# A four-layer stack conditioned on a vector: the lead-in in another order, the keys third, and one reciprocal of the softmax sums per batch

## The chip, the core and the metric

The kernel runs on one core of a Trainium2 chip. The metric is the device time in microseconds. Three runs of the kernel before took 2391.41, 2392.73 and 2393.94 us; the median is 2392.73. All numbers of the trace are from one more execution, the profiled one, of 2394.26 us.

## The reference

x is 4 batches of 512 tokens by 512 channels, with one conditioning vector a batch. Four layers follow each other, all in float32.

```
cond @ W            # 12 blocks of 512 columns: scales and shifts of all layers
layer 0: h = layernorm(x) * (1 + scale) + shift
         q = h Wq (16 heads of 32); c = h Wkd (128); k, v = c Wku, c Wvu (4 heads, each shared by 4)
         rotate q and k; mask: own block of 128, window of 64, every 64th token, no later block
         x += softmax(q k / sqrt(32)) v @ Wo
layer 1: rms norm * scale; 8 heads of 64, one k and v; rotate; no mask; x += attention @ Wo
         x += (silu(h Wg) * (h Wu)) Wd       # 2048 wide
layer 2: 16 heads of 32, normed q and k, added mask; then a GELU MLP, both gated by cond
layer 3: 8 small expert MLPs side by side, norm, silu, output projection
```

## The kernel before

Everything is held with channels (or head channels) on the 128 partitions and tokens along the free axis: a tensor of one batch is four tiles of 128x512. `C`, `TT` and `B` are all 4.

**One woven order.** The program has no loops at run time. Python builds one list of operations (stage, batch, engine, kind, index); each engine runs its own part of the list strictly in order (`Woven`) and waits on the other engines' counters by position. Three parts of it matter here. `lead` holds everything before the first score. `attention01` (`weave`) is the attention of layers 0 and 1, in eight mains: layer 0 for batches 0 to 3, then layer 1. `weave` goes through quads of four score units (16 quads to a batch of layer 0, 8 of layer 1): scores on TensorE into banks 0 to 3, mask and maximum on VectorE (L815), exponential on ScalarE (L845), then transposes ("turn", L909 and L911, in layer 1 L743) into banks 4 and 5, two copies to SBUF on ScalarE (L850) and two on VectorE (L822), and values (L926, L929) into bank 6. Each quad has four points. At them side operations are let in by `sides01`: what prepares the next batch (norm, projections L407, rotations) and the output projection of the last one, spread evenly over the points of the batch.

**Spreading the softmax sums.** After two groups of values, one tile of 128 channels holds four heads (in layer 1 two) and has to be divided by each head's sum. VectorE takes the reciprocals of 16 (8) columns (L827, "recip"). TensorE then makes them a 128x512 tile ("spread", L769): for every block of 128 tokens and every head one full-precision product of a column, broadcast to 32 (64) weights, with the identity. VectorE multiplies (L833, "divide"). This is done four times per batch. A spread takes the next of banks 4 and 5, as a turn does, so the turn after next waits for the divide.

**The lead-in.** `ada` computes the conditioning: 12 blocks (L132; each weight block of 1 MB goes into one of three buffers), a copy of the row on ScalarE (L152), a product that turns it to columns ("turn", L138) and an addition on VectorE (L167). `angles` computes layer 1's rotation tables from the positions: 14 operations on VectorE (L79 to L91), a sine and a cosine on ScalarE (L98). `norm0` is the layer norm of a batch: two sums on GpSimd (L281), the third (L290), a mean on TensorE (L268), centring (L347), squares (L306), sums (L285, L290), variance (L268), logarithm and root (L314, L319), scale (L367) and shift (L331). `proj0` has eight groups: latent, q0 to q3, v, k, near values. `rope0` rotates the key tile and four q tiles: in batch 0 through a product with a permutation (L457), later by two DMAs of SP a tile ("swap", L1885), then a product with the sine on VectorE (L472), one with the cosine and a sum on GpSimd (L484, L490). The list is: angles first; then the whole norm; then blocks 0 and 1 and their turns, and the other blocks folded among projections and rotations.

**Queues.** SP issues in order: block 0, x of batch 0, blocks 1 to 3, block 4, x of batch 1 and so on, each block from the fourth on waiting until TensorE has used the block three before. Then for each batch (b > 0) the swaps of keys and q0, 15 copies that lay the four key heads out to four tiles of four equal strips (L1897), and the swaps of q1 to q3. The first score of a batch waits for all 15 (`k_loaded`). GpSimd issues first: positions, identity and small tables, the biases, layer 0's weights and its rotation tables; then it computes.

## Time and profile before

| | |
|---|---|
| Median of three runs | 2392.73 us |
| Profiled execution, its time | 2394.26 us |
| Its span, first to last instruction | 2392.5 us |
| Busy: TensorE, VectorE, ScalarE, GpSimd | 94%, 49%, 43%, 12% |
| First score | 93.27 us |
| First score of layer 1 | 439.12 us |

The span is the distance between the first and the last instruction on any engine. A full-precision matmul stands as two records; the end of a matmul is modelled, so consecutive ones overlap in the records, and start to start is what one costs in a stream. PE is TensorE, PEld its weight loads, DVE VectorE, ACT ScalarE, POOL GpSimd; a q behind a name is its sequencer. PEclk is the clock that TensorE was granted, as a share of 2.4 GHz. "[7.32 <-DVE sb_nmax L815]" behind a row says that the engine had been idle for 7.32 us before it and that VectorE's L815 ended that.

### The profile page before, as it was taken

What the parts mean: (1) busy time and instruction counts of PE and PEld (TensorE: products, weight loads), DVE (VectorE), ACT (ScalarE), POOL (GpSimd) and SP (SyncE); (2) the same over time, 40 slices, a digit from 0 to 9 for tenths busy, and PEclk for the clock granted to TensorE, in tenths of its full rate; (3) what the DMA queues carried; (4) which work ended last, traced back from release to release, by engine and by line L of the source; (5) the groups of instructions that cost most, each with busy time, mean ns of one, the idle gap of its engine ahead of it and who ended that gap; (6) DMA issues with size and microseconds to landing.
All of it is one profiled execution on the core that took longest, in us unless ns stands there. A gap on an engine that the chain in (4) does not pass through costs nothing.

```text
span 2392.5 us, 34589 instructions
## 1 busy us (share of the span) xinstructions
PE 2246.8 (94%) x14034; PEld 1510.8 (63%) x14034; DVE 1171.0 (49%) x2499; ACT 1034.0 (43%) x2425; POOL 291.3 (12%) x246
## 2 busy tenths in 40 slices
PE   5889999999999999999999989999999899999998
PEld 2455555555555688888887756565654578888633
DVE  2345454454457344443443366667587554544322
ACT  2355555444446221111113266667576552222473
POOL 3331122122021000010000010101010110000021
PEclk9889999999999999999999999999999999999999
DMA  8310020000010002110102211011110101100001
GB/s 275 113 40 27 15 62 28 22 24 18 19 41 27 31 27 84 63 53 27 36 6 82 77 61 64 27 63 36 54 37 19 35 19 36 36 1 1 1 18 53
DMA packets 59487, 104.97 MB, mean 44 GB/s; under 512 B 10592, under 2 KB 24560, under 8 KB 59328
## 3 DMA queue, kind: packets, MB, share of 16 engines
q1 hardware_dynamic: 58368, 100.30, 12.6%
q0 software_dynamic: 960, 2.45, 0.3%
q8 instruction: 111, 1.82, 0.3%
q14 instruction: 48, 0.39, 0.1%
HBM read 77.04 MB, written 10.49 MB: 37 GB/s over the span
## 4 chain that ended last, share of the span: by engine, by line
PE 84%; ACT 7%; DVE 6%; POOL 1%; issue 1%; SPq 1%; DMA 1%; DVEq 0%; POOLq 0%; ACTq 0%
PE banks L1218 36%; PE banks L407 22%; PE banks L743 6%; PE banks L735 4%; PE banks L759 4%; ACT sb_Pr L845 2%; PE banks L769 2%; PE banks L268 2%; ACT sb_PT L850 1%; PE banks L909 1%; DVE sb_hN L367 1%; PE banks L633 1%; PE banks L641 1%; DVE sb_Pr L815 1%; PE banks L893 1%
## 5 line engine op out<-in xcount | busy, mean ns | idle before, releaser
L1218 PE MATMUL banks<-sb_HH,sb_Ws 128*128 128x512 f32 x1536 | 489.4, 392 | 7.6 <-DVE sb_HL L1106 7.6
L1218 PEld LDWEIGHTS banks<-sb_HH,sb_Ws 128*128 128x128 f32 x1536 | 289.3, 188 | 71.2 <-issue 8.1
L1218 PE MATMUL banks<-sb_hidH,sb_Ws 128*128 128x512 f32 x1024 | 330.3, 392 | 0.4 <-DVE sb_x L1289 0.4
L845 ACT ACTIVATE sb_Pr<-sb_Pr,sb_nmax 128x512 f32<-128x512 f32 (+4 forms) x512 | 291.7, 577 | 31.8 <-DVE sb_nmax L815 31.7
L1218 PE MATMUL banks<-sb_HL,sb_Ws 128*128 128x512 f32 x768 | 299.7, 390 | 0.0
L850 ACT ACTIVATE sb_PT<-banks 128x512 f32<-128x512 f32 (+2 forms) x320 | 143.6, 496 | 303.3 <-PE banks L743 226.8
L822 DVE COPY sb_PT<-banks 128x512 f32<-128x512 f32 (+2 forms) x320 | 168.6, 564 | 163.6 <-PE banks L743 109.8
L743 PEld LDWEIGHTS banks<-sb_ident,sb_Pr 128*128 128x128 f32 x1536 | 168.9, 142 | 126.3 <-issue 40.0
L743 PE MATMUL banks<-sb_ident,sb_Pr 128*128 128x128 f32 x1536 | 213.6, 281 | 18.4 <-DVE sb_A L833 5.0
L1218 PEld LDWEIGHTS banks<-sb_hidH,sb_Ws 128*128 128x128 f32 x1024 | 192.2, 188 | 43.8 <-issue 2.3
L1218 PE MATMUL banks<-sb_hidL,sb_Ws 128*128 128x512 f32 x512 | 199.3, 389 | 0.0
L407 PE MATMUL banks<-sb_A,sb_W 128*128 128x512 f32 x384 | 176.6, 603 | 3.8 <-DVE sb_x L1493 2.4
L815 DVE CUSTOM_DVE_ANT_0 sb_Pr<-banks,sb_bias 128x512 f32<-128x512 f32 x256 | 161.5, 687 | 34.5 <-PE banks L735 34.1
L1270 DVE TENSOR_TENSOR sb_tiles<-sb_tiles,banks 128x512 f32<-128x512 f32 x64 | 44.0, 688 | 256.0 <-PE banks L1218 256.0
L1245 ACT ACTIVATE sb_hidH<-sb_tiles 128x512 fp32r<-128x512 f32 x128 | 81.0, 633 | 197.3 <-DVE sb_tiles L1270 195.3
L1218 PEld LDWEIGHTS banks<-sb_HL,sb_Ws 128*128 128x128 f32 x768 | 145.0, 189 | 30.6 <-issue 1.0
L407 PE MATMUL banks<-sb_hN,sb_W 128*128 128x512 f32 x320 | 150.4, 614 | 4.9 <-ACT sb_hN L331 2.8
L735 PE MATMUL banks<-sb_R 32*128 32x512 f32 (+1 forms) x768 | 143.6, 636 | 1.7 <-DVE sb_R L594 0.8
L1240 ACT ACTIVATE sb_tiles<-banks,sb_cols 128x512 f32<-128x512 f32 x64 | 44.1, 689 | 232.2 <-PE banks L1218 232.1
L1289 DVE SCALAR_TENSOR_TENSOR sb_x<-banks,sb_mod,sb_x 128x512 f32<-128x512 f32 x128 | 95.7, 750 | 91.2 <-PE banks L1218 90.9
L1237 ACT ACTIVATE sb_tiles<-banks 128x512 f32<-128x512 f32 x64 | 38.2, 598 | 213.8 <-PE banks L1218 213.8
L759 PE MATMUL banks<-sb_PT,sb_V 128*32 128x256 f32 (+1 forms) x1536 | 127.0, 393 | 0.0
(160 smaller groups left out, 3217.4 us busy)
## 6 DMA issues: line engine op xcount, KB each, us to landing
sb_ring<-split_units SPq DMA_DIRECT2D x48, 512.0 KB, 3.3
sb_ropet<-sb_R SPq DMA_DIRECT2D x70, 128.0 KB, 2.0
sb_staged<-in_L_cond_Wfc SPq DMA_DIRECT2D x16, 512.0 KB, 4.6
sb_wada<-in_L_cond_Wada SPq DMA_DIRECT2D x6, 1024.0 KB, 5.6
split_units<-sb_unitpair SPq DMA_DIRECT2D x12, 512.0 KB, 2.9
sb_x<-in_x SPq DMA_DIRECT2D x4, 1024.0 KB, 9.1
sb_staged<-in_L_cond_Wg SPq DMA_DIRECT2D x8, 512.0 KB, 3.7
sb_staged<-in_L_cond_Wu SPq DMA_DIRECT2D x8, 512.0 KB, 4.7
```

Source lines behind the costliest of these rows:

```text
L268: e.matmul(bank, k.ones[:], k.t1[:, 0, :], start=True, stop=True).then_inc(k.done["pe"], 1)
L407: mm = e.matmul(out, lhsT, rhs, start=start, stop=stop)
L735: mm = e.matmul(bank[:, 0:s.width(u)], s.q(b, c)[rows, i * P:(i + 1) * P], s.k(b, c)[rows, 0:s.width(u)], start=True, stop=True)
L743: mm = e.transpose(bank[:, j * P:(j + 1) * P], k.Pr[:, n % 6, j * P:(j + 1) * P], k.ident[:])
L759: mm = e.matmul(bank[rows, 2 * P * ip + skip:2 * P * (ip + 1)], s.v(b, j, s.vhead(c, hl)), s.PT[:, n % 2, hl, j, skip:2 * P], start=j == 0 ...
L815: ins = e.tensor_tensor_reduce(k.Pr[:, n % 6, 0:s.width(u)], S, s.bias[:, s.units[u][2], 0:s.width(u)], -1.0, 3.0e38, ALU.add, ALU.min, s. ...
L822: ins = e.tensor_copy(*s.turned(k, b, u))
L845: ins = e.activation(prob, prob if s.biased else k.bank(n % 4)[:, 0:s.width(u)], ACT.Exp, bias=s.stat(k, k.nmax, b, u), scale=-1.0 if s.bi ...
L850: ins = e.activation(*s.turned(k, b, u), ACT.Copy)
L1218: mm = e.matmul(bank, lhsT, rhs, start=i == 0, stop=i == len(mats) - 1)
L1245: ins = e.activation(k.hidH[:, st % 2, t, :], k.tile(t), ACT.Copy)
L1289: ins = e.scalar_tensor_tensor(out=k.xs(q, m), in0=s.tab.at[(s.name, b, "down", index)], scalar=1.0 if s.gamma is None else s.gamma(q, m), ...
```

## The change

**Order of the lead-in.** The list is now: sums and block 0; mean; block 1 and turn 0; variance sums; turn 1; block 2; variance; scale and shift; the angle reduction; then a chain of 13 pieces (latent, q0, key, q1, rotation of the key with the sine and cosine tables, q2, rotation of q0, q3, rotation of q1, v, rotation of q2, near values, rotation of q3) with blocks 3 to 11 folded among them. SP loads x of batch 0 first, then blocks 0 and 1, layer 0's weights (before on GpSimd's queue), block 2, the rotation tables (before on GpSimd's queue), the mask, and later blocks; blocks 8 to 11, x of batches 2 and 3 and further weights are issued after batch 0's key copies. The biases have a semaphore of their own, which only the first turn's addition waits for.

**Keys third.** `keys_first` puts the key product third and the key's rotation sixth among the pieces that prepare batches 1 to 3 of layer 0.

**Scores wait by key tile.** There is a semaphore for each of the four key tiles; the first unit of each tile waits for its own copies.

**Reciprocals once per batch.** In layer 0 (all batches) and layer 1 (batches 0 and 1), "recip" and "spread" go. After the last unit of a batch VectorE takes one reciprocal of all 64 (32) columns ("recips") and splits it in a rounded part and the rest. One quad later TensorE transposes the two, 32 columns in all, for each block of tokens ("rows", four transposes), ScalarE copies the 32x512 result as float32r ("rows copy"), and TensorE makes each 128x512 tile by one single-pass product with 32 rows ("wide"): tiles 0 and 1 at the end of that quad, 2 and 3 in the middle of the next. Both kinds use banks 4 and 5. The matrix for it is one more small load (`headsel`), rounded in the lead-in.

```diff
+        elif kind == "rows":
+            for due in after(s.name, b, "rest", 4 // s.per - 1):
+                e.wait_ge(*due)
+            bank = s.tab.claim(e, s, b, kind, u, after)
+            for i in range(TT):
+                columns = k.inverses[:, i, :, :].rearrange("p v h -> p (v h)").bitcast(F32)
+                mm = e.transpose(bank[0:32, i * P:(i + 1) * P], columns, k.ident[:])
+        elif kind == "wide":
+            for due in after("headmatrix", 0, "round", 0):
+                e.wait_ge(*due)
+            for due in after(s.name, b, "rows copy", 0):
+                e.wait_ge(*due)
+            bank = s.tab.claim(e, s, b, kind, u, after)
+            mm = e.matmul(bank, k.headsel[0:32, u, :], k.rows[0:32, :], start=True, stop=True)
...
+        elif kind == "recips":
+            for due in after(s.name, b, "exp", s.U - 1):
+                e.wait_ge(*due)
+            ins = e.reciprocal(k.rsum[:, b % 2, 0:s.U], k.sums[:, b % 2, 0:s.U])
+        elif kind in ("rounded", "rest"):
+            per_row = 4 // s.per
+            for due in after(s.name, b, "recips", 0):
+                e.wait_ge(*due)
...
+                    e.wait_ge(*due)
+            src = k.rsum[:, b % 2, 0:s.U].rearrange("p (c i h) -> p i c h", c=C, i=TT)
+            out = [k.inverses[:, :, v, :].rearrange("p i (c h d) -> p i c h d", c=C, h=s.per)[:, :, :, :, u]
+                   for v in range(2)]
+            if kind == "rounded":
+                ins = e.tensor_copy(out[0], src)
+            else:
+                ins = e.tensor_tensor(out[1], src, out[0].bitcast(F32), ALU.subtract)
...
-            for due in after(s.name, b, "spread", u):
-                e.wait_ge(*due)
-            ins = e.tensor_tensor(s.out(b, u), s.out(b, u), s.tab.at[(s.name, b, "spread", u)], ALU.mult)
+            spread = "wide" if b in s.whole else "spread"
+            for due in after(s.name, b, spread, u):
+                e.wait_ge(*due)
+            ins = e.tensor_tensor(s.out(b, u), s.out(b, u), s.tab.at[(s.name, b, spread, u)], ALU.mult)
...
+        elif kind == "rows copy":
+            for due in after(s.name, b, "rows", 0):
+                e.wait_ge(*due)
...
+            ins = e.activation(k.rows[0:32, :], s.tab.at[(s.name, b, "rows", 0)][0:32, :], ACT.Copy)
...
-            if u == 0:
-                e.wait_ge(*s.k_loaded(b))
+            if u % (s.U // C) == 0:
+                e.wait_ge(*s.k_loaded(b, c))
...
+        for h, b, c in wide[3:]:
+            seq.extend([(h, b, "pe", "wide", c), (h, b, "dve", "divide", c)])
+        wide, later = later, []
+        for h, b, c in wide[:1]:
+            seq.extend([(h, b, "pe", "rows", 0), (h, b, "act", "rows copy", 0)])
         for h, b, u in units(t - 1)[3:]:
             if (u + 1) % h.G == 0:
                 g = h.group(u)
                 seq.append((h, b, "pe", "values", g))
                 if g % 2:
-                    seq.extend([(h, b, "act", "out", g // 2), (h, b, "dve", "recip", g // 2)])
+                    seq.append((h, b, "act", "out", g // 2))
+                if g % 2 and b not in h.whole:
+                    seq.append((h, b, "dve", "recip", g // 2))
                     spreads.append((h, b, g // 2))
+                if b in h.whole and (u + 1) == h.U:
+                    seq.append((h, b, "dve", "recips", 0))
+                    seq.extend((h, b, "dve", kind, i) for kind in ("rounded", "rest") for i in range(4 // h.per))
+                    later = [(h, b, c) for c in range(-1, C)]
...
+        for h, b, c in wide[1:3]:
+            seq.extend([(h, b, "pe", "wide", c), (h, b, "dve", "divide", c)])
...
+                       whole=(0, 1, 2, 3))
...
+                       whole=(0, 1))
...
-        start = pre(0, 0, 1, 2)
...
-        lead = [(ada, 0, "act", "silu", 0), (angles, 0, "dve", "reduce", 0), (angles, 0, "act", "sin", 0),
-                (angles, 0, "act", "cos", 0), (angles, 0, "dve", "negate", 0)] + start[0] + sum(blocks[:3], []) + \
-            fold(start[1:], (0, len(start) - 1, blocks[3:])) + [(ada, 0, "act", "scales", 0)] + \
-            [(ada, 0, "dve", "comb", i) for i in range(len(combs))]
+        def keys_first(proj, rope):
+            return [proj[i] for i in (0, 1, 6, 2, 3)] + rope[:1] + [proj[i] for i in (4, 5, 7)], rope[1:]
+        n0, (p0, r0) = pre(0, 0), keys_first(pre(0, 1), pre(0, 2))
+        headmatrix = HeadMatrix(headsel_read, (l_sel, 16))
+        table = [(angles, 0, "act", "sin", 0), (angles, 0, "act", "cos", 0), (angles, 0, "dve", "negate", 0)]
+        chain = [p0[0], p0[1], p0[2], p0[3], p0[5] + table, p0[4], r0[0], p0[6], r0[1], p0[7], r0[2], p0[8], r0[3]]
+        lead = [(ada, 0, "act", "silu", 0)] + \
+            sum([n0[0], blocks[0], n0[2], blocks[1], n0[3], blocks[2], blocks[3], n0[5], n0[6]], []) + \
+            [(angles, 0, "dve", "reduce", 0)] + fold(chain, (0, 12, blocks[4:])) + \
+            [(ada, 0, "act", "scales", 0)] + [(ada, 0, "dve", "comb", i) for i in range(len(combs))] +             [(headmatrix, 0, "dve", "round", 0)]
         sides01 = []
         for m in range(2 * B - 1):
-            late = beats(posts[m - 1]) if m else []
-            sides01.append(([] if m else pre(1, 0)) + pre(m + 1, 1) + among(late, pre(m + 1, 2), pre(m + 2, 0)) + [[]])
+            late = [[]] * (m > 3) + beats(posts[m - 1]) if m else []
+            first, rest = keys_first(pre(m + 1, 1), pre(m + 1, 2)) if m < 3 else (pre(m + 1, 1), pre(m + 1, 2))
+            sides01.append(([] if m else pre(1, 0)) + first + among(late, rest, pre(m + 2, 0)) + [[]])
...
-            for n, (name, j) in enumerate(blocks):
+            def load_x(b):
+                e.dma_start(x[:, :, b, :], xrows[:, :, b, :]).then_inc(l_x[b], 16)
+            def load_block(n):
+                name, j = blocks[n]
                 if n >= 3:
                     done("ada", 0, "block", n - 3)
                 e.dma_start(wada[n % 3][:], rows(name)[:, :, j * D:(j + 1) * D]).then_inc(l_ada[n % 3], 16)
...
+            load_x(0)
+            load_block(0)
+            load_block(1)
+            for dst, name in ((wkd, "L0_cond_Wkd"), (wq0, "L0_cond_Wq")):
+                e.dma_start(dst, rows(name)).then_inc(l_w[0], 16)
+            for dst, name in ((wku, "L0_cond_Wku"), (wvu, "L0_cond_Wvu")):
+                e.dma_start(dst, a[name]).then_inc(l_w[0], 16)
+            load_block(2)
+            for dst, name in ((perm, "perm"), (k.cosr, "cos0"), (k.sinr, "sin0")):
+                e.dma_start(dst[:], a[name]).then_inc(l_rope, 16)
+            e.dma_start(mask_own[:], a["mask0"][0:P, 0:P]).then_inc(l_bias[0], 16)
+            e.dma_start(mask_near[:], a["mask0"][P:].rearrange("(i p) t -> p i t", p=P)).then_inc(l_bias[0], 16)
+            load_block(3)
+            for name, _ in COLS:
+                e.dma_start(col[name], a[name]).then_inc(l_cols, 16)
+            e.dma_start(k.smul[:], a["L2_cond_scale_mul_log"]).then_inc(l_cols, 16)
+            e.dma_start(k.strip[:], a["strip"]).then_inc(l_cols, 16)
+            e.dma_start(headsel_read[0:32], a["headsel"]).then_inc(l_sel, 16)
+            for n in (4, 5):
+                load_block(n)
+            load_x(1)
+            for n in (6, 7):
+                load_block(n)
...
-                    if c == C - 1:
-                        e.wait_ge(l_k, 16 * (15 * b + 12))
+                    for before in range(C - 1) if c == C - 1 else ():
+                        e.wait_ge(l_k[before], 64 * (b + 1))
                     for strip in range(4 if c < C - 1 else 3):
                         e.dma_start(k.R[32 * strip:32 * strip + 32, b % 2, 1, c, :], heads[32 * c:32 * c + 32, :])\
-                            .then_inc(l_k, 16)
+                            .then_inc(l_k[c], 16)
                 for g in range(2, 5) if b else ():
                     swap(rope0, b, g)
+                if b == 0:
+                    for n in range(8, len(blocks)):
+                        load_block(n)
+                    load_x(2)
+                    load_x(3)
...
-                e.dma_start(modb[:, t0:t0 + n], a[name]).then_inc(l_first, 16)
-            e.dma_start(wkd, rows("L0_cond_Wkd")).then_inc(l_w[0], 16)
-            e.dma_start(wq0, rows("L0_cond_Wq")).then_inc(l_w[0], 16)
-            e.dma_start(wku, a["L0_cond_Wku"]).then_inc(l_w[0], 16)
-            e.dma_start(wvu, a["L0_cond_Wvu"]).then_inc(l_w[0], 16)
-            e.dma_start(perm[:], a["perm"]).then_inc(l_rope, 16)
-            e.dma_start(k.cosr[:], a["cos0"]).then_inc(l_rope, 16)
-            e.dma_start(k.sinr[:], a["sin0"]).then_inc(l_rope, 16)
+                e.dma_start(modb[:, t0:t0 + n], a[name]).then_inc(l_modb, 16)
...
...
```

Left out: the new places of the small buffers in SBUF, the mask in two parts, the constant `headsel`, and the waits for a buffer's last reader.

## Rows read from the trace of the kernel before

**Rows 1.** The page, busy time of TensorE and its share.

```profile
PE 2246.8 (94%) x14034; PEld 1510.8 (63%) x14034; DVE 1171.0 (49%) x2499; ACT 1034.0 (43%) x2425; POOL 291.3 (12%) x246
```

**Rows 2.** Windows: lead-in, layer 0 attention, layer 1 (span, busy us per engine, clock, DMA).

```profile
0.00:93.30 93.30, 61.57 (x272) 27.86 (x272) 25.92 (x53) 20.82 (x34) 32.83 (x40) 0.94 0.76 249
93.30:439.10 345.80, 309.68 (x3434) 190.29 (x3434) 173.39 (x732) 191.58 (x711) 79.92 (x63) 0.94 0.10 31
439.10:1061.00 621.90, 608.85 (x3139) 407.76 (x3140) 295.53 (x458) 212.96 (x482) 85.94 (x72) 1.00 0.12 39
```

**Rows 3.** Timeline 0 to 50: start, duration, engine, line, [idle before].

```profile
11.72 0.43 DVE L79 CAST sb_A<-sb_A 128x512 f32<-128x512 int32 x1 [10.46 <-DMA sb_A<-in_pos]
...
14.47 3.36 POOL L281 TENSOR_TENSOR sb_t<-sb_x 128x512 f32<-128x512 f32 x2 [3.17 <-DMA sb_x<-in_x]
...
21.89 1.94 PE L132 MATMUL banks<-sb_wada,sb_cond 128*32 128x512 f32 x8 [6.52 <-DMA sb_wada<-in_L_cond_W_ada]
...
22.39 1.15 ACT L98 ACTIVATE sb_table<-sb_A 128x512 f32<-128x512 f32 x2 [17.64 <-DVE sb_A L91]
...
29.45 2.08 PE L268 MATMUL banks<-sb_t,sb_ones 128*128 128x512 f32 x2
...
43.84 5.37 PE L407 MATMUL banks<-sb_hN,sb_W 128*128 128x512 f32 x8 [1.82 <-ACT sb_hN L331]
```

**Rows 4.** Timeline 49 to 94.

```profile
49.14 1.06 PE L132 MATMUL banks<-sb_wada,sb_cond 128*32 128x512 f32 x8
...
51.05 3.68 PE L407 MATMUL banks<-sb_hN,sb_W 128*128 128x512 f32 x8
...
71.93 1.10 PE L407 MATMUL banks<-sb_t,sb_W 128*128 128x512 f32 x2
...
74.95 2.10 PE L407 MATMUL banks<-sb_W,sb_t 128*64 128x128 f32 x12
...
76.97 1.12 PE L457 MATMUL banks<-sb_R,sb_perm 128*128 128x512 f32 x2
...
80.89 10.79 SPq L1897 DMA_DIRECT2D sb_R<-sb_R  x15
...
93.27 0.81 PE L893 MATMUL banks<-sb_R 32*128 32x128 f32 x8 [6.78 <-DMA sb_R<-sb_R]
```

**Rows 5.** A window of full DMA queues; the last column is GB/s.

```profile
12.00:36.00 24.00, 14.34 (x58) 5.94 (x58) 13.34 (x22) 6.36 (x11) 7.10 (x5) 1.00 1.04 370
```

**Rows 6.** DMA issues to 100 us: size, median us to landing.

```profile
sb_wada<-in_L_cond_Wada SPq DMA_DIRECT2D x6, 1024.0 KB, 5.6
```

**Rows 7.** Windows after two standstills, the clock behind POOL.

```profile
93.30:109.00 15.70, 13.78 (x116) 9.71 (x120) 8.54 (x40) 10.64 (x39) 5.90 (x5) 0.51 0.01 2
166.60:177.00 10.40, 10.37 (x114) 7.62 (x118) 5.18 (x28) 7.11 (x27) 10.04 (x8) 0.50 0.07 27
```

**Rows 8.** Timeline at the start of batch 1.

```profile
147.02 0.63 DVE L472 TENSOR_TENSOR sb_ropet<-sb_ropet,sb_sin 128x512 f32<-128x512 f32 x1
...
163.01 56.51 SPq L1885 DMA_DIRECT2D sb_ropet<-sb_R  x10
...
165.67 0.69 DVE L472 TENSOR_TENSOR sb_ropet<-sb_ropet,sb_sin 128x512 f32<-128x512 f32 x1 [8.29 <-DMA sb_ropet<-sb_R]
...
166.63 1.21 PE L893 MATMUL banks<-sb_R 32*128 32x128 f32 x6 [7.32 <-DVE sb_nmax L815]
```

**Rows 9.** Groups by line, 93.3 to 439.1: count, busy, mean ns, idle before.

```profile
L769 PE MATMUL banks<-sb_ident,sb_rsum 128*32 128x128 f32 x480 | 16.9, 284 | 5.3 <-ACT sb_PT L850 5.3
```

**Rows 10.** Who waited for whom, 93.3 to 439.1: us in all, times, longest.

```profile
PE banks L909 <- DVE sb_A L833: 7.7, 13, 1.0
```

**Rows 11.** Timeline, three kinds of products near to the new ones.

```profile
468.01 1.09 PE L743 MATMUL banks<-sb_ident,sb_Pr 128*128 128x128 f32 x8
...
900.33 0.61 PE L1218 MATMUL banks<-sb_HH,sb_Ws 128*128 128x512 f32 x2
...
1333.29 0.50 PE L537 MATMUL banks<-sb_rootparts,sb_spread 32*128 32x512 f32 x1
```

More of the change, by code:

```diff
@@ L714, in scored, with masked @@
         return "scores"
+    def masked(s, u):
+        return s.bias[:, s.units[u][2], 0:s.width(u)]
     def column(s, c, i, hl):
@@ L773, in reader @@
     def reader(s, kind, u):
-        return {"scores": (s.released, u), "turn": ("copy", u), "spread": ("divide", u), "values": ("out", u // 2)}[kind]
+        return {"scores": (s.released, u), "turn": ("copy", u), "spread": ("divide", u), "values": ("out", u // 2),
+                "rows": ("rows copy", 0), "wide": ("divide", u)}[kind]
     def copy_waits(s, e, k, b, u, after):
@@ L822, in dve @@
             ins = e.tensor_copy(*s.turned(k, b, u))
+        elif kind == "recips":
[6 more added lines that the diff above has]
+                e.wait_ge(*due)
+            for p, pb in s.tab.rows_of[(s.name, b)]:
+                for due in after(p.name, pb, "rows", 0):
+                    e.wait_ge(*due)
+            if kind == "rest":
+                for due in after(s.name, b, "rounded", per_row - 1):
+                    e.wait_ge(*due)
[6 more added lines that the diff above has]
+                ins = e.tensor_tensor(out[1], src, out[0].bitcast(F32), ALU.subtract)
         elif kind == "recip":
@@ L850, in act @@
             ins = e.activation(*s.turned(k, b, u), ACT.Copy)
+        elif kind == "rows copy":
+            for due in after(s.name, b, "rows", 0):
+                e.wait_ge(*due)
+            for p, pb in s.tab.rows_of[(s.name, b)]:
+                for due in after(p.name, pb, "wide", C - 1):
+                    e.wait_ge(*due)
+            ins = e.activation(k.rows[0:32, :], s.tab.at[(s.name, b, "rows", 0)][0:32, :], ACT.Copy)
         else:
@@ L858, in act, with __init__, dve @@
         ins.then_inc(k.done["act"], 1)
+class HeadMatrix:
+    name = "headmatrix"
+    def __init__(s, source, loaded):
+        s.source, s.loaded = source, loaded
+    def dve(s, k, e, b, kind, index, after):
+        e.wait_ge(*s.loaded)
+        e.tensor_copy(k.headsel[0:32], s.source[0:32]).then_inc(k.done["dve"], 1)
 class NearHeads(Heads):
@@ L1039, in soft @@
             seq.append((h, b, name, kind, u))
-    spreads = []
+    whole = [(h, b) for h, b in mains if b in h.whole]
+    tab.rows_of.update({(h.name, b): whole[i - 1:i] if i else [] for i, (h, b) in enumerate(whole)})
+    spreads, later, wide = [], [], []
     for t in range(-1, len(quads) + 2):
@@ L1071, in weave @@
         copy(t, 3)
+        for h, b, c in wide[1:3]:
+            seq.extend([(h, b, "pe", "wide", c), (h, b, "dve", "divide", c)])
         point(m)
         point(m)
-    assert not spreads and seen[len(mains)] >= len(closing)
+    assert not spreads and not later and seen[len(mains)] >= len(closing)
     return seq
@@ L1395, in conditioned_stack @@
         Y = place("Y", 0, [P, 3, C, T])
-        mask0 = place("mask0", 8192, [P, TT, 200])
-        VN = place("VN", 8992, [P, 2, 3, P])
+        mask_own = place("maskown", 29312, [P, P])
+        mask_near = place("masknear", 8192, [P, TT - 1, 200])
+        VN = place("VN", 8792, [P, 2, 3, P])
+        headsel_read = place("headselread", 9560, [P, C, P])
+        k.headsel = place("headsel", 9560, [P, C, P], F32R)
+        k.inverses = place("inverses", 10072, [P, TT, 2, 16], F32R)
+        k.rows = place("rows", 5632, [P, T], F32R)
         high = lambda b, c: HH[b][:, c, :]
@@ L1406, in conditioned_stack @@
         l_first, l_rope, l_cols, l_cond = sem("l_first"), sem("l_rope"), sem("l_cols"), sem("l_cond")
-        l_ada = [sem(f"l_ada{i}") for i in range(3)]
+        l_sel = sem("l_sel")
+        l_ada, l_modb = [sem(f"l_ada{i}") for i in range(3)], sem("l_modb")
         k.s_angle, l_wo0 = sem("s_angle"), sem("l_wo0")
@@ L1415, in conditioned_stack @@
         l_wq1 = sem("l_wq1")
-        l_k = sem("l_k")
+        l_k = [sem(f"l_k{c}") for c in range(C)]
         k.l_swap = [sem(f"l_swap{i}") for i in range(2)]
@@ L1788, in conditioned_stack @@
         tab = Kit()
-        tab.units, tab.groups, tab.group_number = [], [], {}
+        tab.units, tab.groups, tab.group_number, tab.rows_of = [], [], {}, {}
         first, parts, start = ahead(mlp1)
@@ L2070, in _constants @@
     o["lesser"] = -(np.arange(P) % 32 // 4 == 1).astype(f)[:, None]
+    o["headsel"] = np.tile(np.kron(np.eye(16), np.ones((1, 32))), (2, 1)).reshape(32, C, P).astype(f)
     o["sel"] = np.concatenate([np.eye(32, B, dtype=f)] * 4)
```

57 lines of the change are left out of this document (26 added, 31 removed).

## The prediction

> **What bounds the kernel now.** I read the busy shares first: TensorE works 94% of the span [rows 1], so only what takes work or idle time from TensorE counts. Then the stretches: the lead-in up to the first score (0 to 93.3 us) has TensorE at 61.6 of 93.3 us, attention of layer 0 (to 439.1) at 309.7 of 345.8, and layer 1 with the start of its MLP at 98% [rows 2]. Both halves of the change lie in the first two, where TensorE has 32 and 36 us of slack; what they free moves the rest forward whole, because the rest is TensorE-bound.
>
> In the lead-in the timeline shows the order, not the work, as the bound. x of batch 0 is there at 14.47 us, but its mean product runs at 29.45, behind two condition blocks, the second of which waited for its load until 21.89, and behind rows that ScalarE could copy only after the sine at 22.39, which waits for the angle reduction that VectorE began at 11.72 [rows 3]. The first projection starts at 43.84 [rows 3]. The key tile is rotated only at 76.97, and spread by 15 copies that SP issues from 80.89 on in 10.8 us; TensorE stands still for 6.78 us until 93.27 [rows 4].
>
> **The lead-in, step by step.** Block 0 no longer waits for the last of the biases, only for its weights, and x goes first in SP's queue. The chip moved 370 GB/s when loads were queued [rows 5]. SP's order is now x, block 0, block 1 (1.05 MB each), four weights (1.45 MB), block 2 (1.05 MB). Counting 0.3 MB/us up to 8 us (an estimate under the 370, for GpSimd's small transfers beside them) and 0.37 after, from 3.3 us: x at 7, block 0 at 10, block 1 at 13, block 2 at 20 to 22. The seven weight and table DMAs leave GpSimd's queue, which is free before x lands, and cost SP about 0.5 us each, ahead of what the transfers allow anyway.
>
> GpSimd's two sums of 3.36 us [rows 3] and the third of 1.3, from 7.5, give 12.2. TensorE at half rate, as there: block 0 to 12, mean (2.1) to 14.3, block 1 (1.9) to 16.3, two turns (3.6) to 20, block 2 to 24 at most, var (2.1) to 26, then logarithm, root, first scale and shift about 3 us, less 1 if the clock or the load is early. First projection near 28 instead of 43.84.
>
> From there to the key's rotation: latent 5.4 at the low clock [rows 3], three pairs of block and turn (49.14 to 51.05, 1.9), q0 and q1 at 3.6, key 1.0 [rows 4]: 5.4 + 5.7 + 7.2 + 1.0 = 19.3. Rotation at 47.3, and with the 3.9 from 76.97 to 80.89 the keys are added at 51.2. The angle reduction lies on VectorE behind the scales now, from 30 to 41 at most; it holds up the reading of one turn's bank, which is claimed again only at the rotation, so I cost it at nothing; without that cover, up to 10 us.
>
> What is late next is a queue. SP issues blocks 8 to 11 only after the 15 copies: block 8 at 51.2 + 10.8 = 62, landed 5 us later (5.6 is the median of six) [rows 6], at 67. TensorE reaches it after the rotation (1.1), block 6 and turn, q2, block 7 and turn, a rotation: 47.3 + 1.1 + 1.9 + 3.6 + 1.9 + 1.1 = 57. It stands still for 10 us, with q3, v and the near values behind it. Blocks 9 to 11 land in time. After it: four pairs 7.6, last turn 1.0, q3 3.6, v 1.0, near values 2.0 [rows 4], three rotations 3.3: 18.5. After a standstill of 6.78 us [rows 4] the clock was at 1.2 GHz for the next 15.7 us, and for 10.4 us after one of 7.32 (0.51 and 0.50 of 2.4 GHz) [rows 7, 8], so it will be low here too: at least as for the product of 5.37 against 3.68 [rows 3, 4], 1.7 us, at most half of the 15.7, 8; dense products are nearer to the first, I take 3. First score at 67 + 18.5 + 3 = 88.5: 4.8 gained, not 15. But it comes warm. TensorE was busy 13.8 of those 15.7 us [rows 7], at full rate 6.9 less; ScalarE was busy 10.6 and would hold it up, so I take 4.5. Against it: the last rotation is now directly ahead of the scores, GpSimd begins batch 1's sums after it, and their mean product waits some 2 us. Lead-in: -4.8 - 4.5 + 2, **-7**. Scores that wait by key tile gain nothing in batch 0, where the copies are done by 64. Ends: -19 (no standstill, first score at 76) and +5 (low clock throughout).
>
> **From batch 0 to batch 1.** After the key's sine at 147.02 come 15 copies, then the swap of q1, issued at 163.01; VectorE waited 8.29 us for it, in order, with the softmax behind it, and TensorE 7.32 [rows 8], with two shorter waits just ahead of it 9.7 in all; then it was busy for all of 10.4 us at half clock [rows 7]. At full rate that is 5.2 less; GpSimd was busy 10.0 of them with rotations and sums, so I take 3. With keys third, the key's sine is 4 of 28 side pieces earlier, at 64/28 points each and 4 points to a quad 2.3 quads, some 10 us; q1's stays. From the one to the other were 10.4 us when the wait began and 18.65 were needed [rows 8]; now there are some 20. -9.7 - 3, **-12.5** (ends -6 and -14). No other batch has a wait of VectorE for a swap.
>
> **The spreads.** A spread in layer 0 is 16 products with 128x32 weights; 15 of them fill 16.9 us of the stretch, 1.13 each, or 1.0 without the last one's end, under which the next product starts. The wait ahead of them is 5.3 us in all [rows 9], and 7.7 more go to turns that wait for a division, since a spread takes a turn's bank [rows 10]. Layer 1's, eight products with 64 columns, I take at 0.95. New: four transposes, like the four of 1.09, 0.95 without the end, and four single-pass products at a pitch of 0.22 (two take 0.61; one of the same shape 0.50 with its end) [rows 11], 0.9, together 1.85 per batch. Layer 0: 4 x (4.0 - 1.85) = 8.6; layer 1: 2 x (3.8 - 1.85) = 3.9. The waits I take as equal, (5.3 + 7.7) / 15 x 4 = 3.5 per batch: the wide products take the turn banks too, now two and two, each pair with 1.4 us of divisions on VectorE, the second behind four maxima. VectorE loses four short reciprocals and gets one longer and two to four short operations; even. **-12** (ends -30 with all waits gone, +6 if each burst waits three more). The later divisions come before the output projection, which stands some five quads into the next batch.
>
> By passes alone, which the Trainium skill gives ("FP8 and Floating Point Precision", TensorE Precision Notes: full FP32 takes four passes), a spread would be estimated at 16 x 4 x 128 columns, against 0.22 us for 512, or 3.5 us, and the six batches (16 spreads of that and 8 of half) would give some -60 in place of -12. The rows say 1.0: products in different column groups run beside each other, and this rule oversizes the gain; it gets 1 in 100, within B.
>
> **Sum.** -7 - 12.5 - 12 = -31.5. The profiled execution took 2394.26 us (span 2392.5), so 2362.8; the median of the runs is 1.5 lower: **2361**.
>
> **Rivals.** Within 0.2% (4.8 us) is what a measurement of this kernel can't tell from no change.
> A, the forecast, 0.50: 2353 to 2368.
> B, the copies don't hold block 8 back: first score at 76 to 80, 9 to 12 more: 2350. For it, a single copy is issued in 0.6 and the rest is a wait; against, block 8 stands plainly behind all of them. 0.14.
> C, q1's swap is late still, the margin is 2 us: 6.5 back, 2368. 0.12.
> D, the loads land later than I count (small columns lie between blocks 3 and 4) and the clock stays low through the 18.5: first score at 98, 2371 to 2377. 0.12.
> E, gains and stalls cancel: the first projection comes only near 40 and C holds; within 4.8 of before. 0.06.
> F, slower: the burst at a batch's end. Rows, two wide products and divisions, then two more hold both turn banks; if VectorE is behind by then, TensorE idles 3 us, the clock falls, and the following ten run at half, 5 more: 8 in six batches are +48, less 31: 2409. It decides from standstills like the 7.32; against it, a turn waited 7.7/13 = 0.6 us for a division [rows 10]. 0.06.
>
> Range 2346 to 2378: it leaves out E, F and the tails of B and D. Faster is A to D, 0.88; same 0.06; slower 0.06.
>
> **What would show it.** First projection near 28; keys added near 51; TensorE waiting for a condition block's load for about 10 us, to 67, and the low clock after it; first score near 89 with no wait for copies; no wait of VectorE for a swap at batch 1; 24 single-pass products in place of 24 spreads, with waits for divisions of about 3 us at each batch's end; layer 0's stretch shorter by 20 or more. It is wrong if block 8 holds nothing up, if the low clock covers batch starts, or if that stretch shrinks by less than 10.

## The result and the profile after

The kernel after takes 2372.66 us (median of 4 runs, 2368.46 to 2374.88), the kernel before 2392.92: a ratio of 0.991 [0.9896, 0.9925], or 20.3 us less. The forecast was 2361 with a range of 2346 to 2378, so the time is in the range and the gain two thirds of the 31.5 us forecast. The profiled execution (2368.46, span 2366.7) is the shortest of the four; against the profiled one of before it gains 25.8.

First the page's busy times and the windows of the lead-in, of layer 0's attention and of layer 1 (columns as in [rows 2]).

```profile
PE 2231.2 (94%) x13442; PEld 1492.4 (63%) x13442; DVE 1169.9 (49%) x2498; ACT 1039.6 (44%) x2433; POOL 286.2 (12%) x239
```

```profile
0.00:92.90 92.90, 64.64 (x268) 28.07 (x268) 19.86 (x45) 23.62 (x36) 23.70 (x29) 0.83 0.76 250
97.60:114.00 16.40, 14.26 (x128) 9.94 (x128) 8.57 (x40) 12.39 (x44) 5.92 (x5) 0.61 0.01 1
97.00:418.00 321.00, 295.18 (x2971) 178.57 (x2971) 171.39 (x725) 192.34 (x714) 80.47 (x63) 0.96 0.11 33
418.00:1038.00 620.00, 606.60 (x3001) 401.95 (x3002) 298.75 (x465) 214.19 (x484) 85.73 (x72) 1.00 0.12 39
```

The reader is to see three things. The lead-in is as long as it was (92.9 to the first score, 93.3 before, [rows 2]), though its first projection starts 14.5 us sooner. Layer 0 is shorter: from its first maximum (a row's largest score, taken by VectorE) to layer 1's it takes 322 us in place of 346. From first score to first score it is 325 in place of 346, because 4.6 us now lie between the first score and its maximum, and 1.0 did before. Layer 1 is 620 in place of 622. I also use milestones: the starts of the instructions that write VectorE's maxima (`sb_nmax`) in order, one per unit (a head and its rows; 64 to a batch in layer 0, 32 in layer 1). The first maximum comes at 97.5 us (before: 94.3), the 65th, batch 1's first, at 173.9 (184.6), the 129th at 257.3 (270.8), the 193rd at 338.8 (354.1), layer 1's first at 419.4 (440.5). So the change loses 3.2 us in the lead-in, gains 13.9 in batch 0 and its end, and then 2.9, 1.8 and 5.8 in the three batches after it.

The lead-in in the timeline (start, duration, engine, line; in brackets the idle time before and who ended it). SPq is SyncE's queue issuing DMAs.

```profile
12.24 1.94 PE L133 MATMUL banks<-sb_wada,sb_cond 128*32 128x512 f32 x8 [12.24 <-DMA sb_wada<-in_L_cond_W_ada]
14.11 2.08 PE L269 MATMUL banks<-sb_t,sb_ones 128*128 128x512 f32 x2
...
29.32 6.59 PE L408 MATMUL banks<-sb_hN,sb_W 128*128 128x512 f32 x8 [3.07 <-ACT sb_hN L332]
...
49.65 1.10 PE L458 MATMUL banks<-sb_R,sb_perm 128*128 128x512 f32 x2
...
53.56 10.91 SPq L2014 DMA_DIRECT2D sb_R<-sb_R  x15
...
64.51 1.16 SPq L1969 DMA_DIRECT2D sb_wada<-in_L_cond_Wada  x2
...
70.01 1.93 PE L133 MATMUL banks<-sb_wada,sb_cond 128*32 128x512 f32 x8 [10.79 <-DMA sb_wada<-in_L_cond_Wada]
...
73.60 6.64 PE L408 MATMUL banks<-sb_hN,sb_W 128*128 128x512 f32 x8
...
91.88 1.10 PE L458 MATMUL banks<-sb_R,sb_perm 128*128 128x512 f32 x2
...
92.91 0.48 PE L960 MATMUL banks<-sb_R 32*128 32x128 f32 x2
...
93.62 2.23 DVE L178 TENSOR_TENSOR sb_comb<-sb_mod,sb_cols 128x16 f32<-128x16 f32 x6
...
95.89 1.12 DVE L178 TENSOR_TENSOR sb_comb<-sb_comb,sb_mod 128x16 f32<-128x16 f32 x1
...
96.94 0.41 DVE L921 CAST sb_headsel<-sb_headselread 32x512 fp32r<-32x512 f32 x1
...
97.27 0.27 DVE L836 CUSTOM_DVE_ANT_0 sb_Pr<-banks,sb_maskown 128x128 f32<-128x128 f32 x1
```

The first projection is 14.5 us earlier than before ([rows 3]: 43.84) and the key's rotation 27 us ([rows 4]: 76.97). Then TensorE stands still for 10.79 us before condition block 8, whose load SyncE issued at 64.51, behind the 15 key copies that held its queue for 10.91 us. The product of 73.60 takes 6.64 us in place of 3.68: the clock is at its lower level, as the window over the standstill and what follows it shows (the clock is the column behind POOL's).

```profile
62.60:79.70 17.10, 9.69 (x24) 4.46 (x24) 0.17 (x1) 0.60 (x1) 0.00 (x0) 0.50 0.88 312
```

After the last rotation VectorE computes the seven tables of the modulation and rounds the head matrix, 3.7 us, before the first maximum. In the kernel before the seven tables lay under the wait for the key copies, the 6.78 us up to 93.27 of [rows 4]:

```profile
87.24 1.96 DVE L177 TENSOR_TENSOR sb_comb<-sb_mod,sb_cols 128x16 f32<-128x16 f32 x6
89.23 1.12 DVE L177 TENSOR_TENSOR sb_comb<-sb_comb,sb_mod 128x16 f32<-128x16 f32 x1
```

That wait is gone, and they are late next. TensorE's largest waits in layer 0 (us in all, times, longest), to be read against [rows 10]:

```profile
PE banks L976 <- DVE sb_PT L843: 9.2, 7, 3.6
PE banks L976 <- ACT sb_PT L893: 6.9, 19, 1.0
PE banks L960 <- DVE sb_nmax L836: 5.0, 2, 3.3
```

The turns' wait for divisions (7.7 before) is gone, but the turns wait 16.1 us for the copies of the transposed weights out of the banks (10.6 before). And the products in place of the spreads, against [rows 9]:

```profile
L781 PE MATMUL banks<-sb_rows,sb_headsel 32*128 32x512 f32 x12 | 5.1, 474 | 1.0 <-ACT sb_PT L893 0.5 <-DVE sb_PT L843 0.3
...
L774 PE MATMUL banks<-sb_ident,sb_inverses 128*32 128x128 f32 x12 | 1.8, 275 | 0.5 <-ACT sb_PT L893 0.5
```

### The profile page after: what moved, and what is told of

The parts are those of the page before. It is cut to its first block, busy times and chain, and to the rows that moved or that the text cites. A ratio compares the mean times of both kernels' runs of the same rounds, so it can differ in the third digit from the quotient of the medians.

```text
span 2366.7 us, 33414 instructions
## 1 busy us (share of the span) xinstructions
PE 2231.2 (94%) x13442; PEld 1492.4 (63%) x13442; DVE 1169.9 (49%) x2498; ACT 1039.6 (44%) x2433; POOL 286.2 (12%) x239
## 4 chain that ended last, share of the span: by engine, by line
PE 84%; ACT 7%; DVE 6%; SPq 1%; DMA 1%; issue 1%; POOL 1%; DVEq 0%; ACTq 0%; POOLq 0%
PE banks L1300 36%; PE banks L408 22%; PE banks L749 6%; PE banks L741 5%; PE banks L765 4%; ACT sb_Pr L888 2%; PE banks L269 1%; PE banks L976 1%; DVE sb_hN L368 1%; ACT sb_PT L893 1%; PE banks L634 1%; PE banks L642 1%; DVE sb_Pr L836 1%; PE banks L960 1%; PE banks L789 1%
## 5 line engine op out<-in xcount | busy, mean ns | idle before, releaser
L408 PE MATMUL banks<-sb_hN,sb_W 128*128 128x512 f32 x320 | 156.5, 635 | 6.4 <-ACT sb_hN L332 4.1
```

The lines of the kernel that those rows point to most:

```text
L408: mm = e.matmul(out, lhsT, rhs, start=start, stop=stop)
```

## The experiments

Each kernel is a small edit of the kernel after, timed in five rounds beside the kernel before. "Ratio" is to the kernel before, with its 95% interval of about 0.0013 either way, some 3 us; the difference of two ratios is good to about 4.5 us. Milestones are finer, up to layer 1: two profiles of the same kernel differ there by 1 us at the start of batch 0 and by up to 3.4 later in layer 0. Behind the middle of layer 1 it is over 5.

**The kernel after, again.**

> The changed kernel once more, nothing edited, for the spread of its times beside the next three. Expected 2368 to 2375 us, TensorE waiting 10.8 us for the load of the ninth condition block (index 8).

Measured: 2375.11 (2374.11 to 2375.56), ratio 0.9909 [0.9896, 0.9923]. The 10.8 us wait for block 8 is there again. The first maximum came at 96.5.

**Is it the copies ahead of block 8?** Blocks 8 and 9 are issued by SyncE before the 15 copies.

```
+               for n in (8, 9) if b == 0 else ():
+                   load_block(n)
                done("rope0", b, "add", 0)
                ... 15 copies of the key tile ...
-                   for n in range(8, len(blocks)):
+                   for n in range(10, len(blocks)):
                        load_block(n)
```

> Changed kernel, but SP issues condition blocks 8 and 9 before the 15 key copies. Theory (standstill): the forecast was right that TensorE's 10.8 us before block 8 are bought by SP's order, and the low clock from 62.6 to 79.7 hangs on them. Then the first score comes 13 to 15 us earlier, near 79, and the time falls by 12 to 15, to about 2359. Rival (hidden anyway): other engines or the condition loads give the gain back before batch 1; the time falls by less than 4. Key copies begin about 1 us later in either case.

Measured: 2359.75 (2353.49 to 2362.57), ratio 0.9842 [0.9825, 0.9859], 15.4 us less. The only wait of TensorE for a condition block that is left there is one of 1.42, for block 10 (63.84 is block 9):

```profile
52.72 10.91 SPq L2016 DMA_DIRECT2D sb_R<-sb_R  x15
...
63.84 1.06 PE L133 MATMUL banks<-sb_wada,sb_cond 128*32 128x512 f32 x8
...
69.16 1.07 PE L133 MATMUL banks<-sb_wada,sb_cond 128*32 128x512 f32 x8 [1.42 <-DMA sb_wada<-in_L_cond_emb_W]
```

The first maximum comes at 82.6, 13.9 earlier than in the repeat, and the distance stays between 13.8 and 15.8 us through layer 0. Of the 13.9 the wait (10.8) less 1.4 explains 9.4; the other 4.5 I put down to the lower clock behind the wait. Repeated with later kernels:

> e1's kernel once more, beside e8 and e9 on the same chip: 2359.75 within 3 us, a ratio of 0.984 to 0.986.

Measured: 2362.66 (2356.09 to 2365.51), ratio 0.9855 [0.9834, 0.9876], with the first maximum at 83.7. Against the repeat that is 12.9 us by ratios (16.0 in the first of the two), so the cost of the standstill with its low clock is shown, as some 13 to 16 us.

**Are the tables late next?** First the eight operations were taken to pieces of their own among batch 0's side work.

```
-            [(ada, 0, "act", "scales", 0)] + [(ada, 0, "dve", "comb", i) for i in range(len(combs))] + ...
+            [(ada, 0, "act", "scales", 0)]
+        settled = [[(ada, 0, "dve", "comb", i)] for i in range(len(combs))] + [[(headmatrix, 0, "dve", "round", 0)]]
-            sides01.append(... + among(late, rest, pre(m + 2, 0)) + [[]])
+            sides01.append(... + among(late, rest, pre(m + 2, 0), [] if m else settled) + [[]])
```

> Changed kernel, but VectorE's seven small products of the condition columns (3.35 us) and the rounding of the head matrix (0.41) move from the end of the lead-in in among batch 0's side pieces. Theory (lost cover): before the change they lay under the wait for the key copies; now they stand between the last rotation and the first maximum, and TensorE's 3.35 us behind it bring the low clock back. Then the first maximum comes 3.8 us earlier and the time falls by 4 to 6, to about 2367. Rival (only moved): the pieces cost VectorE the same later, the time stays within 2 us.

> Both edits. Theory: they add, 17 to 20 us less than the changed kernel, about 2353. Rival: the lost cover matters only after the standstill's low clock; then no better than the loads first alone.

The theory missed in both. Measured: 2381.63 (2380.26 to 2383.73), ratio 0.9935 [0.9921, 0.9949], 6.5 slower than the repeat; with the loads first as well 2363.6 (2359.18 to 2372.39), ratio 0.9872 [0.9851, 0.9894], 4 slower than without the tables' move. The first maximum did come 4.3 earlier (92.3), but the 17th is at 122.8 in place of 116.2. The experiment changed two things: 36 pieces in place of 28 bring batch 0's own side pieces forward, and two of them now wait for GpSimd's sums:

```profile
98.01 2.08 PE L269 MATMUL banks<-sb_t,sb_ones 128*128 128x512 f32 x2 [3.32 <-POOL sb_t L291]
...
106.05 2.08 PE L269 MATMUL banks<-sb_t,sb_ones 128*128 128x512 f32 x2 [2.46 <-POOL sb_t L291]
```

So the tables were moved a second way, into VectorE's gaps of the lead-in, each behind the modulation that it reads, with no piece added to batch 0.

```
+        for at, j in ((6, 0), (6, 1), (7, 3), (8, 2), (12, 4), (12, 5), (13, 6)):
+            blocks[at] = blocks[at] + [(ada, 0, "dve", "comb", j)]
+        blocks[10] = blocks[10] + [(headmatrix, 0, "dve", "round", 0)]
```

> The kernel after with the seven products of the modulation tables and the rounding of the head matrix each placed on VectorE in the lead-in right behind the modulation it reads (VectorE waits some 5 us between two of these), not all in a row behind the last rotation; no pieces are added to batch 0. Theory (3.4 us of work stands between the first score and its first maximum): the first maximum comes 3.3 us earlier, 94 in place of 97, TensorE's 3.35 us wait falls to under 0.5, and the time is 2373 - 3.5 = 2369.5 (2368 to 2372). Rival (batch 0's beginning is held by the low clock of its first 17 us, which takes back what the earlier start gives, as with the tables in batch 0): the same time within 1.5 us, unit 16 not earlier than 115.

Measured: 2373.74 (2372.81 to 2375.81), ratio 0.9913 [0.9899, 0.9927]: nothing gained. The first maximum is 4.2 earlier than in the repeat (92.3), the wait of 3.35 is gone, but the 9th is at 103.2 (104.2) and the 17th at 115.3 (116.2). Here is the place, first TensorE, then GpSimd:

```profile
98.05 2.08 PE L269 MATMUL banks<-sb_t,sb_ones 128*128 128x512 f32 x2 [3.13 <-POOL sb_t L291]
```

```profile
91.52 1.27 POOL L485 TENSOR_TENSOR sb_R<-sb_R,sb_cos 128x512 f32<-128x512 f32 x1 [3.28 <-PE banks L458]
92.93 1.27 POOL L491 TENSOR_TENSOR sb_R<-sb_R,sb_ropet 128x512 f32<-128x512 f32 x1
94.16 2.50 POOL L282 TENSOR_TENSOR sb_t<-sb_x 128x512 f32<-128x512 f32 x2
96.73 1.26 POOL L291 TENSOR_TENSOR sb_t<-sb_t 128x512 f32<-128x512 f32 x1
```

The mean product of batch 1 stands among batch 0's turns on TensorE, and it waits for three sums that GpSimd runs only behind its last rotation; they end at 98.0. The forecast had priced this wait at 2 us in the kernel after, where the tables hid it. My rival in the expectation, that the lower clock takes the gain back, named the wrong cause. The test: the sums ahead of the last rotation, in the 3.28 us in which GpSimd waits.

```
-        chain = [..., p0[8], r0[3]]
+        chain = [..., p0[8], pre(1, 0)[0] + r0[3]]
-            sides01.append(([] if m else pre(1, 0)) + first + ...
+            sides01.append(([] if m else [[]] + pre(1, 0)[1:]) + first + ...
```

> The kernel after with the tables' products spread (as e7) and GpSimd's three sums of batch 1 ahead of its last rotation, the loads as in the kernel after. Theory: the 3.13 us wait of the mean's product in e7 goes, unit 8 at 100 to 101 (e7: 103.2, after: 105.1), time 2370 (2368 to 2372), so that all of the 4 us that the first maximum was brought forward are kept. Rival (the low clock of the stretch from 97 us takes it back): 2373, as e7.

Measured: 2367.93 (2363.39 to 2370.51), ratio 0.9879 [0.9861, 0.9897]. The mean product waits for nothing, the 9th maximum is at 100.2 and the 17th at 110.8, 3.0 and 4.5 earlier than with the tables alone, and the distance is 4.5 at layer 1's first. The second is more than the wait: in the window 90 to 114 us the clock was 0.86 here and 0.72 there. The loads first and the tables spread, without and with the sums ahead:

> Blocks 8 and 9 issued ahead of the 15 key copies (as in e1) and the tables' products spread in the lead-in (as in e7), no piece added to batch 0. If the two act by themselves: first maximum at 78 to 79 us, unit 8 at 89, and 2359.75 - 1.3 = 2358.5 (2356 to 2360), since in e7 only 1.3 of the 4.3 us at the first maximum were left at unit 8, the rest lost in a 3.13 us wait of the mean's product for GpSimd's sums, which should be seen here again. If the tables' place decides with the earlier clock (other theory), the gain is the whole 4 us: 2355.5.

> As e8, and GpSimd's three sums of batch 1's x (two of 1.25 and one of 1.27 us) put ahead of its last rotation of batch 0, into its 3.3 us wait. Theory (the mean's product of batch 1 waits for these sums once the tables are out of the way): no wait of the mean's product for GpSimd, unit 8 some 2.5 to 3 us earlier than in e8, time 2358.5 - 3 = 2355.5 (2353 to 2358). Rival (the last rotation, now some 3 us later, holds the scores of heads 12 to 15): unit 16 as in e8, the same time within 1.5 us.

Measured: without the sums 2359.32 (2357.14 to 2361.47), ratio 0.9844 [0.9828, 0.986], no better than the loads alone, with the wait of 3.3 us for GpSimd; with them **2353.9** (2347.42 to 2356.37), ratio 0.9818 [0.9799, 0.9838], the fastest kernel of this study, 42.1 under the kernel before beside it. Against the loads alone the gain of the other two moves is less certain: by ratios it is 5.7 and 8.9 us (the loads-first kernel was timed twice), the first of these within the noise of two ratios. In the profiled executions the 17th maximum is 2.4 and 3.0 us earlier than in the two with the loads alone, but layer 1's first is 1.1 and 2.4 later (405.6 against 404.5 and 403.2). GpSimd in the fastest kernel, with the sums before the rotation:

```profile
77.65 2.48 POOL L282 TENSOR_TENSOR sb_t<-sb_x 128x512 f32<-128x512 f32 x2 [2.18 <-PE banks L408]
80.21 1.27 POOL L291 TENSOR_TENSOR sb_t<-sb_t 128x512 f32<-128x512 f32 x1
81.44 1.27 POOL L485 TENSOR_TENSOR sb_R<-sb_R,sb_cos 128x512 f32<-128x512 f32 x1
```

**The three terms of the forecast, each undone alone.** The spreads per tile as before (`whole=()` in both layers):

> The kernel after with the divisions and their spreads in layer 0 and layer 1 done per tile as before (whole=() for all batches); the key-first order, the lead-in and the loads stay. Theory 1 (the spreads' term of the forecast, 12 us, is right): 2373 + 12 = 2385 (2381 to 2389), the loss spread over batches 0 to 3 of layer 0 and the first two of layer 1, about 2 us each, the first score where it was. Rival (the spreads were hidden behind the softmax anyway, as TensorE is not what the quads wait for): within 3 us of the kernel after, 2372 to 2376.

Measured: 2382.29 (2376.95 to 2384.91), ratio 0.9946 [0.9933, 0.996], by ratios 8.9 us slower than the repeat (0.0037 of 2393, give or take 4.5). Against the kernel after the loss is 2.3 at batch 1's first maximum, 3.1 and 4.8 at the next two batches' and 14.1 at layer 1's; from there to the 321st maximum it grows by 1.5, against the repeat it falls by 0.2. The 9.3 us of the last batch are more than its spreads cost. Its granted clock was 0.94 (0.98 in the kernel after), and TensorE waited there for layer 1's weights, a wait that neither profile of the kernel after has:

```profile
351.12 5.37 PE L408 MATMUL banks<-sb_hN,sb_W 128*128 128x512 f32 x8 [2.04 <-DMA sb_W<-in_L_cond_Wq]
```

With the product at 5.37 in place of 3.67, that alone is 3.7 us. With one profile I can't say whether the spreads brought it about.

The old order of projections in batches 1 to 3:

```
-            first, rest = keys_first(pre(m + 1, 1), pre(m + 1, 2)) if m < 3 else ...
+            first, rest = keys_first(pre(m + 1, 1), pre(m + 1, 2)) if m < 0 else ...
```

> The kernel after with the old order of projections in batches 1 to 3 of layer 0 (keys last but for batch 0), all else kept. Theory 1 (the stall at the start of batch 1, 12.5 us in the forecast, is taken away by the order): 2373 + 12.5 = 2385 (2381 to 2388), VectorE waits some 8 us for the swapped half of the keys again near 159 us from the start, and the loss stands whole at unit 64. Rival (the wait goes by the key tiles' separate waits and not by the order): under 4 us, 2373 to 2377.

Measured: 2388.37 (2378.74 to 2391.24), ratio 0.9965 [0.9953, 0.9977], 13.4 slower by ratios. The wait for the swap is back, and TensorE's behind it:

```profile
167.23 0.69 DVE L473 TENSOR_TENSOR sb_ropet<-sb_ropet,sb_sin 128x512 f32<-128x512 f32 x1 [9.45 <-DMA sb_ropet<-sb_R]
...
168.18 1.21 PE L960 MATMUL banks<-sb_R 32*128 32x128 f32 x6 [8.03 <-DVE sb_nmax L836]
```

Against the kernel after, 10.2 us of it stand at batch 1's first maximum and 14.7 at layer 1's. The lead-in as before (its list and the order of both DMA queues), the rest changed:

> The kernel before's lead-in (its list of projections and rotations for batch 0, its order of loads on SyncE's and GpSimd's queues), with the spreads and the key-first order of batches 1 to 3 of the kernel after. Theory 1 (the new lead-in costs about 3 us, as the first maximum came at 97.5 us in place of 94.3): 2373 - 3 = 2370 (2367 to 2373). Rival (the new lead-in gave its forecast 7 us later on, in batch 0): 2380. With 2370, the whole gain of the change comes from the stall and the spreads.

Measured: 2372.56 (2371.18 to 2375.21), ratio 0.9909 [0.9894, 0.9923]: the same as with the new lead-in. Its first maximum comes at 91.1, 3.1 earlier than in the kernel before. The reason is a part of the change that I had given nothing: scores that wait for their own key tile only. With the copies still being issued, the first score runs:

```profile
84.42 7.79 SPq L2005 DMA_DIRECT2D sb_R<-sb_R  x10
...
86.75 0.48 PE L960 MATMUL banks<-sb_R 32*128 32x128 f32 x2
...
91.27 1.21 PE L960 MATMUL banks<-sb_R 32*128 32x128 f32 x6 [3.07 <-DVE sb_nmax L836]
```

That is 6.5 us before the 93.27 of [rows 4], of which 3.4 are lost again behind the tables. The 3.1 that are left don't last either. The 9th maximum is only 0.8 earlier than in the kernel before and the 17th 0.3, because here too the mean product of batch 1 waits for GpSimd's sums:

```profile
95.98 2.07 PE L269 MATMUL banks<-sb_t,sb_ones 128*128 128x512 f32 x2 [2.03 <-POOL sb_t L291]
```

## Why the prediction was right, and where it was not

**The lead-in's order: right up to the standstill.** First projection 29.32 (forecast 28), its duration 6.59 (5.4), the key's rotation 49.65 (47.3), keys added 53.5 (51.2), block 8 issued 64.5 and landed 70.0 (62 and 67), TensorE idle 10.79 (10). Only the clock's price was taken too small: the product 6.64 in place of 3.68, block and turn each some 0.8 more, 4.5 in all by the loads-first runs (3). First score 92.91 (88.5): 3.0 of the 4.4 from block 8's landing and 1.4 from the clock.

**The lead-in's total: failed.** Forecast -7, measured 0 against the old lead-in with the same rest, and +2 to +3 at layer 1's first maximum. The step that failed is "it comes warm", -4.5. The stretch behind the first maximum ran at 0.61 of the clock (0.51 before, [rows 7]), and from the first to the 17th maximum took 19.6 us, where the kernel before took 19.1: none of the 4.5 is there. TensorE stood still again just ahead of it, 3.35 us behind the tables, which the forecast had not listed among what was late next. The trace before had them, in the shadow of the 6.78 us wait. The forecast asked what is late next on SyncE's queue and not on VectorE's. Whether the 3.35 us brought the low clock is open. With the tables spread and the sums ahead the clock from 90 to 114 us was 0.86, against 0.72 in the kernel after. But with the loads first as well, the stretch from 79 to 100 us has a clock of 0.67 (TensorE busy 17.87 of 21 us), and so have the two kernels with the loads first where one of the waits is still there. So it would not have come warm without that wait either. And the +2 for GpSimd's sums was a right wait in the wrong kernel: it is 0 in the kernel after, 3.1 as soon as the tables are gone, and 2.0 with the old lead-in.

**Scores by key tile, forecast at nothing: right for the kernel after** (no wait for copies, first score 1.0 us behind the last rotation), and yet worth 6.5 us at the first score with the old lead-in. Of that 3.1 is left at the first maximum and 0.3 at the 17th, so in the end nothing was near enough. It was never undone alone.

**Batch 0 to 1: right.** Forecast -12.5, measured -13.4 by ratios. VectorE waits for no swap. By milestones 10.2 come at the swap and the rest in the batches after it, where I had forecast nothing; what brings it there was not followed up.

**The spreads: right in size, by two errors that cancel.** Forecast -12, of it 8.6 of TensorE's own work in layer 0; the waits, 3.5 a batch, I took to stay. Measured -8.9 by ratios, -13 to -14 by milestones in layer 0 (3.7 of it the wait for layer 1's weights and the slow product behind it, in that one execution) and nothing measurable in layer 1 (forecast -3.9). TensorE's rows in layer 0, before against after, give a like sum. The stretch of before holds 15 of 16 spreads, 16.9 us [rows 9], the one of after 12 of 16 new products and their rows, 5.1 + 1.8; for all sixteen 18.0 and 9.2, so 8.8 less, as forecast. The waits for spreads and divisions, 5.3 + 7.7 [rows 9, 10], or 13.9 for sixteen, became 1.0 + 0.5 and another 1.3 of turns waiting for ScalarE's copy of the rows (L900), or 3.7 for sixteen. But those for copies of the transposed weights grew by 5.5, from 7.6 + 3.0 to 9.2 + 6.9. So 4.7 of the waits went, and 8.8 + 4.7 = 13.5. The profile of the kernel after has no wait for a division, where the forecast expected some 3 us at each batch's end.

An estimate by the rule of the Trainium skill ("FP8 and Floating Point Precision", TensorE Precision Notes: four passes for full FP32) had -60 for this term. The run with the old spreads shows 8.9. As a price of products in different column groups the rule is too high by a factor of three, 3.5 us a spread where the rows have 1.13.

**Sum.** 0 - 13.4 - 8.9 = -22.3 by the three runs that undo one part each, against 0.991 and 0.9909, or -21.5 and -21.8. The parts add up within their noise, which for three such differences is some 8 us. The forecast gain was some 10 us too high, and the lead-in's 7 and 3 of the spreads' are where it went (its three terms, unrounded, give 32.5 and not 31.5). That the time still fell inside the range is in part luck: 2372.66 lies outside the 2353 to 2368 of A, the forecast proper, and inside the band of D, for a reason that is only half D's. Of the rivals, B (the copies don't hold block 8) is refuted by the 10.79 us row, C by the swap that is no longer waited for, E by the first projection at 29.32, F by the missing waits for divisions. D was half there: the clock stayed low for 17 us around the standstill and the loads landed 3 us late, but the first score came at 93, not 98.

## What to carry to other kernels

When a reorder takes away a wait, list for each engine what lay under that wait in program order; the work that was free there (here 3.7 us of small tables on VectorE, then 3.8 us of sums on GpSimd) is what comes next, one after the other, and moving only the first of them gained nothing. SyncE issues its DMAs in order: loads with a near deadline go ahead of a burst of small copies, and here two lines moved were worth 13 to 16 us, while the whole new lead-in without them measured the same as the old one. Undo each part alone before you believe the sum, and follow a gain beyond the first milestone: 3.1 us at the first maximum were 0.3 at the 17th.

## What the runs showed of the hardware

Fifteen copies within the core's memory held SyncE's queue for 10.91 us (10.79 in [rows 4]). It is two things. The first twelve were issued at one per 0.63 us; the last three began only at 62.70, because the program makes SyncE wait there until the first twelve have landed:

```profile
53.56 7.61 SPq L2014 DMA_DIRECT2D sb_R<-sb_R  x12
...
62.70 1.77 SPq L2014 DMA_DIRECT2D sb_R<-sb_R  x3
```

So some 9.4 us are issuing and 1.5 are that wait. A 1 MB block took no longer to issue than a copy (two in 1.16 us at 64.51). The Trainium skill ("DMA: Bandwidth & Descriptors", Issuing engines are not separate DMA queues) calls the time to initiate a DMA "usually small relative to the DMA itself". For these copies it was not: most took 0.59 us to issue and landed some 2.0 us after their issue began, and the fifteen follow one another. Undoing their place in the queue gave 15.4 us.

Seven products of 128x16 in a row on VectorE took 3.35 us, the last of them 1.12 alone. Placed elsewhere the same instruction took 0.17. What made them slow is GpSimd. The last product ends when the GpSimd sum beside it ends; so does one of them that the first try had put in the middle of batch 0:

```profile
95.70 1.28 POOL L282 TENSOR_TENSOR sb_t<-sb_x 128x512 f32<-128x512 f32 x1
95.89 1.12 DVE L178 TENSOR_TENSOR sb_comb<-sb_comb,sb_mod 128x16 f32<-128x16 f32 x1
```

```profile
166.04 1.27 POOL L485 TENSOR_TENSOR sb_R<-sb_R,sb_cos 128x512 f32<-128x512 f32 x1
166.44 0.92 DVE L178 TENSOR_TENSOR sb_comb<-sb_mod,sb_cols 128x16 f32<-128x16 f32 x1
```

It is so in all 14 profiles of this study. They hold 98 of these table products. Each of the 43 that took longer than 0.25 us ends 0.03 us after the end of a GpSimd instruction; the other 55 took 0.16 to 0.18 us, and none of those lies wholly inside a GpSimd instruction. The fastest kernel has one that seems to run beside GpSimd's sums and yet took 0.17:

```profile
78.80 0.17 DVE L178 TENSOR_TENSOR sb_comb<-sb_comb,sb_mod 128x16 f32<-128x16 f32 x1
```

It stands where the first sum of 77.65 ends, at 78.91, and the second begins. That a product reads what was written just before it is not the reason: in the same kernel two at 75.72, right behind the modulation that the first of them reads and with GpSimd idle, took 0.26 together. So most of the tables' 3.35 us is waiting for GpSimd's last rotation and sums. A kernel that keeps only those two apart was not run.

And around TensorE's standstill of 10.79 us the granted clock was at half, 1.2 GHz, for 17.1 us, 9.69 of them busy with products.
